# Decoder layer in float32: feed-forward products in plain float32 in place of two 12-bit parts, four buffers for transposes and activations, and a new order at the end

## The reference

```
x = x + attention(layernorm(x))            # 16 heads of 16, softmax / 16, W_qkv and W_out with biases
x = x + cross_attention(layernorm(x), ctx) # 16 heads of 16 over 64 keys
x = x + ffn(layernorm(x))

def ffn(x):
    h = x @ ternary(W_fc).T                # 256 -> 1024
    h = gelu(h)
    h = layernorm(h) * ln_w + ln_b         # over 1024
    return h @ ternary(W_proj).T           # 1024 -> 256

def ternary(W):                            # -1, 0 or 1
    g = mean(abs(W)) + 1e-6
    return sign(W / g) * minimum(round(abs(W / g)), 1)
```

## Time and profile before

| | us |
|---|---|
| median of 3 runs | 1230.46 (1229.64 to 1232.3) |
| the profiled execution | 1228.81 |
| its span, first to last instruction | 1226.9 |
| PE busy in the span | 1155.1 |
| DVE busy | 1049.5 |
| ACT busy | 833.3 |
| POOL busy | 294.0 |
| mean granted TensorE clock | 0.985 of full speed |

### The profile page before, as it was taken

The page is one execution under the profiler, slowest core; times in us unless marked ns, Lnnn a source line. Parts: engine busy times, 40 slices in busy tenths (PEclk is TensorE's granted clock), DMA queues, the critical chain, the costliest instruction groups (busy, mean ns, idle before and its releaser), DMA issues.

```text
span 1226.9 us, 18450 instructions
## 1 busy us (share of the span) xinstructions
PE 1155.1 (94%) x6476; PEld 587.1 (48%) x6476; DVE 1049.5 (86%) x1974; ACT 833.3 (68%) x1386; POOL 294.0 (24%) x404
## 2 busy tenths in 40 slices
PE   5989979999999999999999999998889999999995
PEld 3644333333333333333333333334558677778775
DVE  4688769999999999999999999984699999898875
ACT  4321558877777777777777777774687778778852
POOL 2120301101110110111011000011565465445421
PEclk9999889999999999999999999998999999999998
DMA  4873773303322330430332200023110211100001
GB/s 154 249 229 138 136 168 62 58 15 53 58 39 29 62 54 10 63 57 19 49 58 45 30 11 6 6 69 103 59 35 21 69 61 36 43 18 18 1 18 35
DMA packets 45532, 74.95 MB, mean 61 GB/s; under 512 B 10112, under 2 KB 23296, under 8 KB 45440
## 3 DMA queue, kind: packets, MB, share of 16 engines
q0 software_dynamic: 9792, 27.80, 13.9%
q1 hardware_dynamic: 35648, 45.97, 12.5%
HBM read 47.53 MB, written 25.69 MB: 60 GB/s over the span
## 4 chain that ended last, share of the span: by engine, by line
PE 74%; DVE 15%; issue 3%; ACT 3%; DMA 2%; POOL 1%; SPq 1%; DVEq 0%; ACTq 0%; POOLq 0%
PE ps L1234 21%; PE ps L1353 20%; PE ps L1197 15%; DVE maxes L841 10%; PE ps L1512 4%; PE ps L1432 4%; PE ps L1339 3%; PE ps L1497 2%; PE ps L1441 2%; ACT prob L616 1%; PE ps L1451 1%; DMA Qs<-mt 1%; DVE xhat L1092 1%; DVE maxes L834 1%; PE ps L1401 1%
## 5 line engine op out<-in xcount | busy, mean ns | idle before, releaser
L841 DVE TENSOR_REDUCE maxes<-ps 128x1 f32<-128x512 f32 x968 | 609.2, 684 | 62.9 <-PE ps L1234 62.9
L616 ACT ACTIVATE prob<-ps 128x1024 f32<-128x1024 f32 x512 | 495.8, 1021 | 156.6 <-PE ps L1339 153.8
L1234 PE MATMUL ps<-Ks,Qs 48*128 48x512 f32 x1024 | 364.0, 476 | 17.8 <-DVE maxes L834 2.6
L1234 PEld LDWEIGHTS ps<-Ks,Qs 48*128 48x128 f32 x1024 | 143.6, 184 | 360.0 <-DVE maxes L841 323.6
L1353 PE MATMUL ps<-prob,V_all 128*32 128x512 f32 x2048 | 274.5, 608 | 0.7 <-ACT prob L616 0.6
L1339 PE MATMUL ps<-Qs,Ks 50*128 50x512 f32 x1024 | 239.1, 413 | 9.9 <-DMA Qs<-mt 6.6
L329 POOL DMA_DIRECT2D Qs<-qk_scratch x90 | 44.2, 499 | 494.7 <-PE ps L1353 454.5
L1339 PEld LDWEIGHTS ps<-Qs,Ks 50*128 50x128 f32 x1024 | 134.8, 188 | 26.3 <-ACT prob L616 11.6
L683 ACT ACTIVATE pe_<-ps,nmx 128x64 f32<-128x64 f32 x512 | 109.8, 365 | 8.1 <-DVE nmx L1011 8.0
L540 POOL TENSOR_TENSOR pe_<-pe_,rsum 128x512 f32<-128x512 f32 x64 | 66.6, 1052 | 59.3 <-DVE rsum L1028 59.3
L1512 PE MATMUL ps<-t_p,fT 128*128 128x256 f32 x512 | 76.9, 293 | 0.0
(11 more groups left out here) (116 smaller groups left out, 1238.9 us busy)
## 6 DMA issues: line engine op xcount, KB each, us to landing
qk_scratch<-parts SPq DMA_DIRECT2D x32, 512.0 KB, 3.3
Qs<-qk_scratch POOLq DMA_DIRECT2D x90, 128.0 KB, 5.1
Ks<-qk_scratch POOLq DMA_DIRECT2D x90, 128.0 KB, 7.6
xa<-in_x POOLq DMA_DIRECT2D x8, 512.0 KB, 5.1
o_scratch<-ot SPq DMA_DIRECT2D x128, 32.0 KB
on_raw<-o_scratch SPq DMA_DIRECT2D x8, 512.0 KB
r_raw<-r_scratch SPq DMA_DIRECT2D x16, 256.0 KB
x_in<-in_x SPq DMA_DIRECT2D x8, 512.0 KB, 4.2
```

The lines of the kernel that those rows point to most:

```text
L616: act.activation(prob[:, par, h].rearrange("p a q -> p (a q)"), ps[:, 2 * h:2 * h + 2, :].rearrange("p a q -> p (a q)"), ACT.Exp).then_inc ...
L841: dve.tensor_reduce(maxes[:, qc, j * BLK + blk, half:half + 1], ps[:, MAX_BANK["tile", t], :], AX.X, ALU.max).then_inc(max_reduced, 1)
L1234: pe.matmul(ps[:, bank, :], stack(Qs[g], j, STACK, slice(q0, q0 + P)), stack(Ks[g], j, STACK, slice(half * 512, (half + 1) * 512)), start= ...
```

## The change

Both feed-forward products take plain float32 operands: xn3T and fT have one part in place of two, and x3_low and ft_low on DVE are gone, with their places in DVE's list. x3_high becomes x3_copy and ft_high becomes ft_copy, which write float32 and release the consumers themselves. fc has 2 matmuls for each half and f_proj 1 for each block, in place of 4 and 2. gl gets four buffers (gelu waits for the f_apply of four blocks before), fT four places in all chunks. The bank of a transpose is as before. In the loops the order of what remains is unchanged. In the end section PE does f_proj(END-1, 4 to 7) behind fc(END, 3) where they stood between the fc blocks; DVE does f_stats(END, 2) ahead of f_apply(END, 1), and f_out(END-1) behind f_apply(END, 3); POOL does x2_plus_b(END) ahead of the rstd_f of END and behind a wait for xn3_ready.

```diff
--- before.py
+++ after.py
@@ -31,6 +31,7 @@
 CH = 512
 NCH = T // CH
 END = NCH - 1
+FT_PLACES = 4
 BLK = CH // P
 KT = E // P
 HG = 4
@@ -87,7 +88,7 @@
 
 def ft_bank(c, t):
 
-    return ((4, 5, 0, 1)[t % 4], t % 4) if c == END else (4 + t % 2, t % 2)
+    return (4, 5, 0, 1)[t % 4] if c == END else 4 + t % 2
 
 
 HALF = MAXT // 2
@@ -209,7 +210,7 @@
         x2_f = sb("x2_f", [P, 2, BLK, E])
         xn_1 = sb("xn_1", [P, BLK, E])
         xn_2 = sb("xn_2", [P, BLK, E])
-        xn3T = sb("xn3T", [P, 2, KT, CH])
+        xn3T = sb("xn3T", [P, KT, CH])
         q2T = sb("q2T", [P, KT, CH])
         nmx = sb("nmx", [P, 2 * BLK, 8])
         pe_ = sb("pe_", [P, 2 * BLK, CH])
@@ -217,12 +218,12 @@
         psum = sb("psum", [P, 2 * BLK, 8])
         rsum = sb("rsum", [P, 2 * BLK, 8])
         o2T = sb("o2T", [P, KT, CH])
-        gl = sb("gl", [P, 2, F])
+        gl = sb("gl", [P, 4, F])
         fstats = sb("fstats", [P, 2, 2, 6])
         fmv = sb("fmv", [P, 2, 2])
         fveps = sb("fveps", [P, 2])
         frstd = sb("frstd", [P, 2])
-        fT = sb("fT", [P, 4, 2, CH])
+        fT = sb("fT", [P, FT_PLACES, CH])
         xo = sb("xo", [P, BLK, E])
 
 
...
@@ -579,9 +578,10 @@
                 x_plus_b(c + 2)
 
             rstd_3(END)
+            pool.wait_ge(xn3_ready, NCH)
+            x2_plus_b(END)
             for blk in range(BLK):
                 rstd_f(END, blk)
-            x2_plus_b(END)
 
 
         @block.scalar
@@ -702,59 +702,56 @@
                     act.wait_ge(o2_done, 2 * c)
                 act.activation(o2T[:, m, :], ps[:, BANK["val", c, m], :], ACT.Copy).then_inc(o2_copied, 1)
 
-            def x3_high(c, k):
+            def x3_copy(c, k):
                 if not 0 <= c < NCH:
                     return
                 act.wait_ge(t3_done, 2 * c + k + 1)
                 if c:
                     act.wait_ge(fc_done, BLK * c)
-                act.activation(xn3T[:, 0, k, :].bitcast(F32R), ps[:, BANK["t3", c, k], :], ACT.Copy).then_inc(t3_high, 1)
+                act.activation(xn3T[:, k, :], ps[:, BANK["t3", c, k], :], ACT.Copy).then_inc(t3_copied, 1)
 
             def gelu(c, blk):
                 if not 0 <= c < NCH:
                     return
                 n = BLK * c + blk
                 act.wait_ge(fc_done, n + 1)
-                if n >= 2:
-                    act.wait_ge(xhat_done, n - 1)
+                if n >= BLK:
+                    act.wait_ge(xhat_done, n - BLK + 1)
                 r = fc_bank(c, blk)
-                act.activation(gl[:, blk % 2, :], ps[:, r:r + 2, :].rearrange("p a q -> p (a q)"),
+                act.activation(gl[:, blk, :], ps[:, r:r + 2, :].rearrange("p a q -> p (a q)"),
                                ACT.Gelu).then_inc(gelu_done, 1)
 
-            def ft_high(c, t):
+            def ft_copy(c, t):
                 if not 0 <= c < NCH:
                     return
                 n = HT * c + t
                 act.wait_ge(hT_done, n + 1)
-                if c == END and t >= 4:
-                    act.wait_ge(fp_done, n - 3)
-                elif n >= 2 and not (c == END and t >= 2):
-                    act.wait_ge(fp_done, n - 1)
-                r, place = ft_bank(c, t)
-                act.activation(fT[:, place, 0, :].bitcast(F32R), ps[:, r, :], ACT.Identity,
-                               scale=ln_w[:, t:t + 1]).then_inc(fh_ready, 1)
+                if n >= FT_PLACES:
+                    act.wait_ge(fp_done, n - FT_PLACES + 1)
+                act.activation(fT[:, t % FT_PLACES, :], ps[:, ft_bank(c, t), :], ACT.Identity,
+                               scale=ln_w[:, t:t + 1]).then_inc(ft_ready, 1)
 
...
@@ -774,17 +771,17 @@
                 c_exp(c + 1, 0)
 
             for t in range(5):
-                ft_high(END - 1, t)
-            x3_high(END, 0)
-            x3_high(END, 1)
-            ft_high(END - 1, 5)
-            ft_high(END - 1, 6)
+                ft_copy(END - 1, t)
+            x3_copy(END, 0)
+            x3_copy(END, 1)
+            ft_copy(END - 1, 5)
+            ft_copy(END - 1, 6)
             gelu(END, 0)
-            ft_high(END - 1, 7)
+            ft_copy(END - 1, 7)
             for blk in range(1, BLK):
                 gelu(END, blk)
             for t in range(HT):
-                ft_high(END, t)
+                ft_copy(END, t)
 
         @block.vector
         def _(dve):
@@ -950,7 +947,7 @@
                 dve.tensor_scalar(neg.bitcast(F32R), wf, thr[:, 2, i:i + 1], None, ALU.is_lt).then_inc(prep_done, 1)
                 n += 1
                 dve.wait_ge(prep_done, n)
-                dve.scalar_tensor_tensor(out=ternary[:].rearrange("p k n -> p (k n)").bitcast(F32R), in0=wf,
+                dve.scalar_tensor_tensor(out=ternary[:].rearrange("p k n -> p (k n)"), in0=wf,
                                          scalar=thr[:, 1, i:i + 1], in1=neg,
                                          op0=ALU.is_gt, op1=ALU.subtract).then_inc(prep_done, 1)
                 n += 1
@@ -1062,21 +1059,13 @@
                                           ALU.subtract, ALU.mult)
                 i.then_inc(xn3_ready, 1)
 
-            def x3_low(c):
-                if not 0 <= c < NCH:
-                    return
-                for k in range(KT):
-                    dve.wait_ge(t3_high, 2 * c + k + 1)
-                    dve.tensor_tensor(xn3T[:, 1, k, :].bitcast(F32R), ps[:, BANK["t3", c, k], :], xn3T[:, 0, k, :],
-                                      ALU.subtract).then_inc(t3_low, 1)
-
             def f_stats(c, blk):
                 if not 0 <= c < NCH:
                     return
                 n, k = BLK * c + blk, blk % 2
                 dve.wait_ge(gelu_done, n + 1)
                 for h in range(2):
-                    i = dve.bn_stats(fstats[:, k, h, :], gl[:, k, h * 512:(h + 1) * 512])
+                    i = dve.bn_stats(fstats[:, k, h, :], gl[:, blk, h * 512:(h + 1) * 512])
                 i.then_inc(fstats_done, 1)
                 dve.wait_ge(fstats_done, n + 1)
                 dve.tensor_copy(touch[:], fstats[:, k, 0, 0:1])
@@ -1089,17 +1078,8 @@
                 dve.wait_ge(frstd_ready, BLK * c + blk + 1)
                 if c:
                     dve.wait_ge(hT_done, HT * c)
-                dve.tensor_scalar(xhat[:, blk, :], gl[:, k, :], fmv[:, k, 0:1], frstd[:, k:k + 1],
+                dve.tensor_scalar(xhat[:, blk, :], gl[:, blk, :], fmv[:, k, 0:1], frstd[:, k:k + 1],
                                   ALU.subtract, ALU.mult).then_inc(xhat_done, 1)
-
-            def ft_low(c, t):
-                if not 0 <= c < NCH:
-                    return
-                dve.wait_ge(fh_ready, HT * c + t + 1)
-                r, place = ft_bank(c, t)
-                dve.scalar_tensor_tensor(out=fT[:, place, 1, :].bitcast(F32R), in0=ps[:, r, :],
-                                         scalar=ln_w[:, t:t + 1], in1=fT[:, place, 0, :],
-                                         op0=ALU.mult, op1=ALU.subtract).then_inc(ft_ready, 1)
 
             def f_out(c):
                 if not 0 <= c < NCH:
@@ -1113,23 +1093,18 @@
                                       x2_f[:, c % 2, 2 * i:2 * i + 2, :], ALU.add).then_inc(out_added, 1)
 
...
-            ft_low(END - 1, 1)
             x2_stats(END)
-            ft_low(END - 1, 2)
             x2_apply(END)
-            ft_low(END - 1, 3)
-            ft_low(END - 1, 4)
-            x3_low(END)
-            ft_low(END - 1, 5)
-            ft_low(END - 1, 6)
             f_stats(END, 0)
-            ft_low(END - 1, 7)
             f_stats(END, 1)
             f_apply(END, 0)
+            f_stats(END, 2)
             f_apply(END, 1)
-            f_out(END - 1)
-            f_stats(END, 2)
             f_stats(END, 3)
             f_apply(END, 2)
             f_apply(END, 3)
-            for t in range(HT):
-                ft_low(END, t)
+            f_out(END - 1)
             f_out(END)
+
 
         @block.tensor
         def _(pe):
@@ -1378,7 +1340,7 @@
             pe.wait_ge(m_copied, HALVES)
 
             freed = {"t2": (t2_copied, 2), "q2": (q2_copied, 2), "s": (exp2_done, 8), "pt": (pt_copied, 8), "val": (o2_copied, 2),
-                     "o2": (x2_added, 2), "out": (x1_added, 2), "t3": (t3_low, 2)}
+                     "o2": (x2_added, 2), "out": (x1_added, 2), "t3": (t3_copied, 2)}
 
             def x_bank(kind, c, i):
 
@@ -1469,7 +1431,7 @@
 
                 if not 0 <= c < NCH:
                     return
-                pe.wait_ge(t3_low, 2 * c + 2)
+                pe.wait_ge(t3_copied, 2 * c + 2)
                 if blk >= 2:
                     pe.wait_ge(gelu_done, BLK * c + blk - 1)
                 elif c and c < END and blk == 0:
@@ -1477,9 +1439,9 @@
                 elif c and c < END and blk == 1:
                     pe.wait_ge(out_added, 2 * c)
                 for h in range(2):
-                    for n, (part, k) in enumerate((part, k) for part in range(2) for k in range(KT)):
```

(78 more changed lines are left out.)

## The result

The changed kernel takes **1315.88 us** (median of 3 runs, 1313.84 to 1315.96) against 1230.46: ratio 1.069, interval 1.0668 to 1.0711. It is slower by 85.4 us; the forecast was 1317, range 1309 to 1328, slower with a chance of 0.96. The profiled execution took 1315.96 us, where the sum of the prediction gave 1315.5.

A forecast was written before the change was run, and what follows sets the result against it. PE was taken as the bound in the steady chunks. Products +100.8 us, end -11.3, waits -1.2, -1.0 and -0.6 gave +86.7: 1315.5 for the profiled execution, 1317 for the median, range 1309 to 1328.

The forecast's parts named there:

- The price of the products: PE's feed-forward products: f_proj 0.945 to 1.725 us, fc block 1.85 to 3.44, together +100.8 us, 12.6 per full chunk.
- the collision: Steady chunks: f_apply takes 2.56 us beside POOL's x_plus_b, 0.76 alone, so PE starts its transposes 0.43 us late.
- The doubling that the Trainium skill's four passes would give: Rival on the feed-forward products: a plain product costs two full pairs, +120 us of products, 1336 us total; chance 0.04.
- DVE's relief is worth nothing by itself: Removing ft_low and x3_low takes 57.5 us off DVE, which counts only where PE stood waiting behind it.
- the plain copies on ACT cost nothing: ACT's copies to plain float32 add 0, bounded by ACT's 10 idle us a chunk for ten copies.
- The end: From END-1's first transpose to the last f_proj: 42.3 us becomes 49.8, +7.5 where products add 18.8, so -11.3.
- the cover of 6.9 us: End section: f_proj 4 to 7 of END-1 keep PE busy 6.9 us, covering an xhat wait shrunk to 5.2.
- The waits in the loop: PE waits regained in the loops: -1.2 us in the first fc chunk, -1.0 in four steady chunks, -0.6 in the last pass.
- The sum: Whole kernel: +100.8 - 11.3 - 1.2 - 1.0 - 0.6 = +86.7 us, giving 1315.5 for the profiled execution.
- the other three waits (0.63, 0.62, 0.56): PE waits to vanish: 0.63 us for x3_low's bank and 0.62 for q2T (first fc chunk), 0.56 for ft_low (last pass).

The follow-up runs named there:

- e8: The kernel before plus one wait on POOL that starts x_plus_b only after both x2_half of two chunks earlier: 1229.1 us, ratio 0.9992.
- e3: The changed kernel with fc back in two reduced parts, f_proj left plain: 1268.0 us, ratio 1.0303 to before.
- e6: The changed kernel with both feed-forward products as one reduced product each, low parts left out: 1190.4 us, ratio 0.9688 to before.
- e5: The changed kernel with unused DVE work put back where ft_low and x3_low stood in the loop: 1316.15 us, ratio 1.0702 to before.
- e4: The changed kernel with the old end order on PE, DVE and POOL: 1324.1 us, ratio 1.0759 to before.
- e1: The kernel before with the new buffers and end order but still two-part products: 1224.1 us, ratio 0.9946.
- e2: The kernel before with four gl buffers and four fT places alone, old end order: 1230.05 us, ratio 0.9992.
- e7: The kernel before with new buffers, new end order, two-part products and a POOL wait delaying x_plus_b: 1220.85 us, ratio 0.9926.

## Why the prediction was right

**The price of the products: right.** The bound was read as PE in every steady period, and the price as start-to-start distances of like products elsewhere in the same trace. The period without the collision is 43.23 (e8) and 55.86 after: +12.63, predicted 12.60. e3 takes the fc half back out for 47.9 us, 50.9 less the waits that return. The doubling that the Trainium skill's four passes would give (FP8 and Floating Point Precision, TensorE Precision Notes) didn't come: a pair became 1.83 and 1.86 times as long, and against a single reduced product e6 measured 3.63, not 4. That doesn't speak against four passes as such: a quarter of the plain product is 0.108 us, and the reduced product, which the prediction's reckoning took for one such pass, takes 0.119.

**DVE's relief is worth nothing by itself: right** (e5). What pays in the loops is that PE no longer waits for ft_low and x3_low, which the prediction counted apart. And the plain copies on ACT cost nothing (ACT busy 833.0 after, 833.3 before).

**The end: right**, -11.3 (+7.5 where the products alone add 18.8) for -11.3. PE had the cover of 6.9 us for 5.0 us of xhat chain (predicted 5.2), and the clock stayed up. e4 loses 8.3 of it. The rest, 3.0, comes with the old order too. 2.3 of it show in e4's waits of PE: 6.95 us for xhat in place of 7.78, and 0.3 for the first copy of fT where before had 1.13 and 0.25 for ft_low and 0.41 for xn. The other 0.7 are not assigned.

**The waits in the loop: size about right, reason wrong.** The step "With four gl buffers the last gelu, the last rstd_f and x_plus_b all come 0.5 us earlier against PE, and f_apply ends in time" failed. In e1 and e2, with the buffers and two parts, the wait stands as before: gelu does start earlier, but DVE's f_stats queue up behind x1_apply, so that rstd_f and x_plus_b come no sooner (x_plus_b starts 4.28 us ahead of PE's transpose in e1 as before). e3 has one part of the plain products (f_proj) and the wait as well; only where fc is plain does it vanish. There DVE waits for the last gelu and starts f_stats(3) as it ends (980.35 us; in e1 0.6 us after), and x_plus_b starts 3.7 us after the end of the last fc block in place of 4.2 in e1. That explains how the plain fc hides the wait. The collision itself is still there in the changed kernel, and f_apply(3) is over 0.15 us ahead of the transpose at 987.17:

```profile
982.79 2.35 POOL L503 TENSOR_TENSOR x_b<-x_in,b_out 128x1024 f32<-128x1024 f32 x1
...
983.67 2.03 DVE L1081 TENSOR_SCALAR xhat<-gl,fmv,frstd 128x1024 f32<-128x1024 f32 x1
...
986.22 0.80 DVE L1081 TENSOR_SCALAR xhat<-gl,fmv,frstd 128x1024 f32<-128x1024 f32 x1
```

That it is the wait's cause is what e7 and e8 showed. The gain was 2.0 us in place of the 1.0 taken (its upper bound was put at 1.7).

**The sum.** Up to the end section it is +77.2 against +79.2 forecast. From the first o2 to the first transpose of tile 0 it is +4.8 (forecast +5.2), in the four steady periods +48.5 (+49.4), in the fifth +12.55 (+12.6), and in the last +11.4 (+12.0). Of the 1.9 us that the waits gave back beyond the forecast, 0.9 are the collision's. Another 0.4 are a wait that the prediction overlooked: in the last pass before, PE also stood for x3_low, which held the bank of x_pT(c, 3). From the start of the f_proj at 1161.30 to that transpose are 1.35 us, where an f_proj takes 0.95 (chain of before, in order of time):

```profile
1161.90 0.61 DVE xn3T L1070
1162.51 0.14 issue
1162.65 0.63 PE ps L1441 x4
```

And some 0.4 lie in how the other three waits (0.63, 0.62, 0.56) were sized. They were taken as PE's idle time shown, which begins only when the tail of the piece ahead is over; start to start they are 0.79, 0.70 and 0.72. At xhat the prediction had reckoned with the tail (0.43 for the 0.27 shown). The last 0.2 are not assigned. The 2.4 us that the changed execution was late before the phase went the other way, so it is luck that the profiled time met the sum so closely (1315.96 and 1315.5).

## What to carry to other kernels

Before giving up a split into reduced parts, price both forms in start-to-start distances from the same trace, and count records per product: here two reduced products cost 0.24 us and the plain one 0.43, so on an engine that is the bound, as PE is here, plain loses that difference, and relief of another engine is no counterweight. Judge a mixed change by its parts: the end order alone was worth having, inside a change that lost 85 us. And give every wait its own test before it is put down to a buffer: the same 0.5 us survived two more buffers and went with one semaphore wait.

## What was not expected of the hardware

A 128x1024 f_apply on DVE takes 0.76 to 0.81 us alone and 2.56 to 2.82 beside a POOL pass of 2.35 us that starts just before it, so that it ends some 0.5 us after POOL's pass does. In e8 the added wait held the POOL pass for 4.0 us, until the DVE work was through. That cost nothing and brought 0.50 us a chunk.
